# Attention's weight products 128 rows deep, with zero rows for the other head

## The chip, the cores and the metric

One core of one Trainium2 chip. The metric is the device time of one execution of the kernel in microseconds; lower is better. The time before is 529.92 us, the median of 3 runs (529.62 to 530.06).

## The reference

One layer on x of 2048 tokens by 128 features: a feed-forward part, attention, and a second feed-forward part, each with a layer norm ahead and added to x. The feed-forward part has one shared and eight routed experts of width 256, two experts chosen per token. Attention has 4 heads of 32 features and 64 slots per head. Per head, with the causal mask:

```
wk = exp(clip(slots of k));  zk = cumsum(wk over tokens)
logits = ((q k^T masked) wk) * scale / zk
p = softmax(logits over the 64 slots)
wv = exp(clip(slots of v));  zv = cumsum(wv over tokens)
A[t, s] = sum over the 64 slots m of (p / zv)[t, m] * wv[s, m],  masked
o = A v;  then o is normalised, gated and projected
```

The change concerns the line for A, "the products of the weights". All data stay float32 in this part.

## The kernel before, in words

The feed-forward parts run over experts and groups of 512 tokens. Attention lies between them and runs over 16 chunks of 128 tokens. What lies in earlier chunks is kept in a running state (logits and outputs of earlier tokens come from it), so within a chunk only 128 by 128 products are formed.

The order of work in attention is written out by hand, once per engine: each engine has a function `attn_step(i, n)` that calls the parts of up to four chunks at once, `front` (chunk i), `mid` (i - 1), `last` (i - 2) and `end` (i - 3), as `stages` gives them. Steps 0 to 3 are written out, steps 4 to 15 run in a hardware loop on each engine with two steps in its body (the branch is behind the odd step), and steps 16 to 18 are written out again. Engines meet through semaphores only, and each works off its own list in order.

The parts that matter here, with their lines:

- TensorE, in the order of a step: `project` (L1177 to 1179), `running_sums` (L1259), `turn_v` (L1250, transposes the slots of v, two heads at a time, into PSUM), `slot_logits` (L1219), `turn_o` (L1333), `weights_a` (L1311), `logits_of_earlier` (L1268), `out_proj` (L1338, waits for ScalarE's copy of o), `logits_of_chunk` (L1275), `turn_qk` (L1226 and L1230, wait for the split of q and k to be complete), `outputs` (L1323, L1325), `add_state`, `add_sums`, `scores` (L1241), `turn_p` (L1299).
- ScalarE: `copy_state` (six copies of parts of the rows, L417 and L420), `sums_log` (L394), `copy_value_slots` (L406, the transposed slots of v from PSUM to vslot_t), `sums_first_inverse` (L399), `copy_o` (L452), `qk_high` (L374, L375), `slots_high` (L362), `slots_exponent` (L355), `copy_qk_parts` (L382), `slots_middle` (L367), `soft_exp` (L431), `o_square` (L445), `copy_q` (L387), `copy_p` (L438).
- GpSimd: `rope_add` (L633, L634), `qk_low` (L640, behind L375), `slots_rest` (L617), `slots_low` (L622), `gate_o` (L648), `root_o` (L567).
- VectorE: `rope_multiply` (L870 to 875), `norm_apply` (L990), `clip_slots` (L883), `mask_a` (L953, waits for the products), `sums_product` (L899), `sums_inverse` (L904, writes slot_inv), `add_y` (L997), `soft_scale` (L912), `soft_min` (L918), `norm_shares` (L969), `soft_centre` (L926), `prob_scale` (L934), and the small rest up to `mask_s` (L891).

vslot_t and p_t hold two heads below each other: rows 0 to 63 are the slots of an even head, rows 64 to 127 those of an odd head, and the index a says which pair. `weights_a` multiplies 64 rows at a time, first both even heads, then, behind a wait of TensorE for itself (`a_even`), both odd heads. The four products go side by side into one bank of PSUM. A float32 product shows in the trace as two passes, so a step has eight loads and eight matmuls at L1311.

Of the kernel before, what the change touches and what calls it, by code (L numbers as in the profile page):

```python
# [16 lines left out]
ACT = mybir.ActivationFunctionType  # L17
# [6 lines left out]
P = 128  # L24
# [13 lines left out]
M = 64  # L38
# [49 lines left out]
def macaron_kernel(nc, x_in, consts, w_ffn, w_router, router_bias, w_qkvg, w_low, w_slots, w_out, gnorm, out):  # L88
# [3 lines left out]
    with ExitStack() as ctx:  # L92
        def sb(name, shape, dt=F32):
            return ctx.enter_context(nc.sbuf_tensor(name, shape, dt))

        def sem(name):
            return ctx.enter_context(nc.semaphore(name))
# [22 lines left out]
        zero16 = sb("zero16", [P, HM + 4 * DK], F16)  # L120
# [43 lines left out]
        state = sb("state", [P, 2, HM + 2 * 2 * DK])  # L164
# [10 lines left out]
        prob_inv = sb("prob_inv", [P, 2, H])  # L175
        pz = sb("pz", [P, HM])
        p_t = sb("p_t", [P, 2, 2, P])
        vslot_t = sb("vslot_t", [P, 2, 2, P])
        a_masked = sb("a_masked", [P, H, P])
        o1 = sb("o1", [P, D])  # L180
        o_sq = sb("o_sq", [P, D])
# [20 lines left out]
        state_ps, sum_ps, qk_ps, slots_ps, s_ps, c_ps, vturn_ps, oturn_ps = bank  # L202
# [3 lines left out]
        vslot_t_ps, pz_t_ps = vturn_ps[:, 0:HM], vturn_ps[:, HM:2 * HM]  # L206
        o_t_ps, y_ps = oturn_ps[:, 0:P], oturn_ps[:, P:2 * P]

        def stacked(q_block, k_block):
# [23 lines left out]
        whi0_done, wr_hi_done, wlo0_done = sem("whi0_done"), sem("wr_hi_done"), sem("wlo0_done")  # L233
        names = ("low_turned low_hi_done low_lo_done v_projected v_copied g_projected gate_silu gate_ready "
                 "projected slots_done clip_done slots_exp slots_b1 slots_rest slots_b2 slots_b3 rope_parts qk_done "
                 "qk_hi_done qk_lo_done qk_turned qk_t_copied q_t_copied a_even "
                 "s_done vslot_turned vslot_copied sums_done s_mask_done state_copied logits_done sums_ln sums_guess "
                 "sums_prod sums_inv back_done "
                 "logit_scaled min_done centred prob_done prob_summed pz_done pinv_done pz_turned p_copied "
# [1 line left out]
        S = {n: sem(n) for n in names.split()}  # L241
# [32 lines left out]
        def _(act):  # L274
# [126 lines left out]
            def copy_value_slots(c, p, n):  # L401

                act.wait_ge(S["vslot_turned"], c + 1)
                if n >= 2:
                    act.wait_ge(S["a_done"], c - 1)
                act.activation(vslot_t[:, p, :, :], vslot_t_ps.rearrange("p (a b) -> p a b", a=2), ACT.Copy).then_inc(S["vslot_copied"], 1)  # L406

            def copy_state(c, p, n):

# [44 lines left out]
            def attn_step(i, n):  # L454
                front, mid, last, end = stages(i, n)
                if mid:
                    copy_state(*mid)
                if mid:
                    sums_log(*mid)
                if mid:  # L460
                    copy_value_slots(*mid)
                if mid:
                    sums_first_inverse(*mid)
                if end:
                    copy_o(*end)
                if front:
                    qk_high(*front)
                if front:
                    slots_high(*front)
                if front:  # L470
                    slots_exponent(*front)
                if front:
                    copy_qk_parts(*front)
                if front:
                    slots_middle(*front)
                if mid:
                    soft_exp(*mid)
                if last:
                    o_square(*last)
                if front:  # L480
                    copy_q(*front)
                if mid:
                    copy_p(*mid)
# [46 lines left out]
        def _(pool):  # L530
# [70 lines left out]
            pool.wait_ge(wlo_done, E + 2)  # L601
            nc.gpsimd.memset(low_st[6 * LOW:P, :], 1.0).then_inc(ones_set, 1)
            pool.wait_ge(ones_set, 1)
            for zeros in (state[:, :, :], zero16[:, :]):
                nc.gpsimd.memset(zeros, 0.0)
            nc.gpsimd.tensor_copy(tri16[:, :], tri)
            nc.gpsimd.tensor_copy(rest16[:, :], rest)
# [63 lines left out]
            for g in range(NG):  # L671
                pool.wait_ge(S["gate_silu"], g + 1)
                for c in range(g * GT, (g + 1) * GT):
                    i = nc.gpsimd.tensor_tensor(gates[:, c, :], gate_raw[:, c, :], gn[:, :], ALU.mult)
# [405 lines left out]
        def _(pe):  # L1080
            mm = nc.tensor.matmul
# [220 lines left out]
            def weights_a(c, p, n):  # L1302

                pe.wait_ge(S["p_copied"], c + 1)
                pe.wait_ge(S["vslot_copied"], c + 1)
                if n >= 1:
                    pe.wait_ge(S["o1_done"], c)
                for j, done in enumerate(("a_even", "a_done")):
                    rows = slice(j * M, (j + 1) * M)
                    for a in range(2):  # L1310
                        i = mm(c_ps[:, (2 * a + j) * P:(2 * a + j + 1) * P], vslot_t[rows, p, a, :], p_t[rows, p, a, :], start=True, stop=True)  # L1311
                    i.then_inc(S[done], 1)
                    if j == 0:
                        pe.wait_ge(S["a_even"], c + 1)

            def outputs(c, p, n):

# [22 lines left out]
            def attn_step(i, n):  # L1340
# [11 lines left out]
                if last:  # L1352
                    weights_a(*last)
# [109 lines left out]
```

## Time and profile before

| | |
|---|---|
| median of 3 runs | 529.92 us |
| the profiled execution | 530.72 us |
| its span, first to last instruction | 528.8 us |
| mean granted TensorE clock | 0.957 |
| TensorE (PE) busy | 467.3 us, 88% |
| VectorE (DVE) busy | 427.0 us, 81% |
| ScalarE (ACT) busy | 309.1 us, 58% |
| GpSimd (POOL) busy | 173.3 us, 33% |
| share of L1311 in the chain that ended last | 3% |

The profile is one execution. PE is TensorE's matmuls, PEld its weight loads. Times are us from the start of the span. Busy shares are means over very different stages: attention has another limit than the feed-forward parts. A row of the timeline gives start, duration (from the first start to the last end where instructions are merged), engine, line and operation, output and inputs with their shapes, the count, and in brackets the idle time of the engine ahead of it with what ended it.

### The profile page before, as it was taken

What the parts mean: (1) busy time and instruction counts of PE and PEld (TensorE: products, weight loads), DVE (VectorE), ACT (ScalarE), POOL (GpSimd) and SP (SyncE); (2) the same over time, 40 slices, a digit from 0 to 9 for tenths busy, and PEclk for the clock granted to TensorE, in tenths of its full rate; (3) what the DMA queues carried; (4) which work ended last, traced back from release to release, by engine and by line L of the source; (5) the groups of instructions that cost most, each with busy time, mean ns of one, the idle gap of its engine ahead of it and who ended that gap; (6) DMA issues with size and microseconds to landing.
All of it is one profiled execution on the core that took longest, in us unless ns stands there. A gap on an engine that the chain in (4) does not pass through costs nothing.

```text
span 528.8 us, 12332 instructions
## 1 busy us (share of the span) xinstructions
PE 467.3 (88%) x3895; PEld 318.7 (60%) x3895; DVE 427.0 (81%) x1139; ACT 309.1 (58%) x667; POOL 173.3 (33%) x198
## 2 busy tenths in 40 slices
PE   1788999999999568998898999885889999999996
PEld 0344566666665556676776776764455666666664
DVE  3598999999999835777778777866599999999997
ACT  3543555555555675877777777653555555555553
POOL 2999960000000364566566666534000000000000
PEclk9998999999999785999999999996599999999999
DMA  6212000000000000000000000000000000000002
GB/s 204 90 61 78 1 0 0 0 0 0 0 1 1 1 1 0 2 1 2 0 0 0 0 0 0 0 1 0 2 1 2 0 0 0 0 0 0 0 0 79
DMA packets 6697, 6.98 MB, mean 13 GB/s; under 512 B 818, under 2 KB 5170, under 8 KB 6676
## 3 DMA queue, kind: packets, MB, share of 16 engines
q1 hardware_dynamic: 6532, 6.33, 3.9%
q10 hardware_dynamic: 144, 0.39, 0.2%
q8 instruction: 11, 0.18, 0.1%
q14 instruction: 10, 0.08, 0.1%
HBM read 5.67 MB, written 1.05 MB: 13 GB/s over the span
## 4 chain that ended last, share of the span: by engine, by line
PE 60%; DVE 19%; issue 9%; ACT 7%; POOL 2%; DVEq 1%; DMA 1%; POOLq 0%; ACTq 0%
PE bank L1128 15%; PE bank L1140 10%; PE bank L1141 10%; PE bank L1142 10%; DVE h L804 4%; PE bank L1311 3%; DVE h_lo L810 2%; ACT gate_s L313 2%; PE bank L1325 2%; PE bank L1275 2%; DVE stats L702 2%; DVE pz L934 1%; DVE x L793 1%; DVE logit_c L926 1%; PE bank L1230 1%
## 5 line engine op out<-in xcount | busy, mean ns | idle before, releaser
L318 ACT ACTIVATE h_hi<-h 128x512 f16<-128x512 f32 x144 | 90.7, 630 | 133.3 <-DVE h L804 133.3
L804 DVE SCALAR_TENSOR_TENSOR h<-bank,gate_s 128x512 f32<-128x512 f32 x144 | 99.4, 690 | 28.4 <-ACT gate_s L313 19.0
L1128 PE MATMUL bank<-w_hi,h_hi 128*128 (+1 forms) x576 | 106.4, 221 | 12.9 <-DVE h_lo L810 8.3
L1140 PE MATMUL bank<-xt_hi,w_hi 128*128 128x512 f16 x288 | 111.8, 388 | 0.0
L1141 PE MATMUL bank<-xt_hi,w_lo 128*128 128x512 f16 x288 | 111.7, 388 | 0.0
L1142 PE MATMUL bank<-xt_lo,w_hi 128*128 128x512 f16 x288 | 111.5, 387 | 0.0
L1128 PE MATMUL bank<-w_hi,h_lo 128*128 (+1 forms) x576 | 105.9, 221 | 0.0
L1128 PE MATMUL bank<-w_lo,h_hi 128*128 (+1 forms) x576 | 105.9, 221 | 0.0
L810 DVE TENSOR_TENSOR h_lo<-h,h_hi 128x512 f16<-128x512 f32 x144 | 100.6, 698 | 0.1
L793 DVE SCALAR_TENSOR_TENSOR x<-bank,wts,x 128x128 f32<-128x128 f32 x288 | 86.5, 343 | 1.6 <-PE bank L1128 1.1
L313 ACT ACTIVATE gate_s<-bank 128x512 f32<-128x512 f32 x144 | 83.5, 580 | 0.6 <-PE bank L1142 0.6
L1128 PEld LDWEIGHTS bank<-w_hi,h_hi 128*128 128x128 f16 x576 | 56.6, 98 | 37.4 <-DVE h_lo L810 12.1
L1128 PEld LDWEIGHTS bank<-w_lo,h_hi 128*128 128x128 f16 x576 | 56.8, 99 | 12.4 <-issue 0.3
L1128 PEld LDWEIGHTS bank<-w_hi,h_lo 128*128 128x128 f16 x576 | 56.9, 99 | 0.0
L1142 PEld LDWEIGHTS bank<-xt_lo,w_hi 128*128 (+1 forms) x288 | 28.7, 100 | 35.6 <-issue 3.0
L538 POOL TENSOR_SCALAR var_e<-mv 128x4 f32<-128x4 f32 x12 | 3.4, 284 | 117.9 <-issue 95.1
L1140 PEld LDWEIGHTS bank<-xt_hi,w_hi 128*128 (+1 forms) x288 | 28.7, 100 | 19.5 <-issue 2.5
L1141 PEld LDWEIGHTS bank<-xt_hi,w_lo 128*128 (+1 forms) x288 | 28.7, 100 | 19.0 <-issue 2.2
L953 DVE TENSOR_TENSOR a_masked<-bank,cst 128x512 f32<-128x512 f32 x16 | 11.1, 692 | 20.6 <-PE bank L1311 20.6
L617 POOL TENSOR_TENSOR slot_r<-slots,slot_b 128x512 f32<-128x512 f32 x16 | 23.8, 1485 | 6.7 <-issue 6.3
L622 POOL TENSOR_TENSOR slot_b<-slot_r,slot_b 128x512 bf16<-128x512 f32 x16 | 20.5, 1282 | 15.8 <-ACT slot_b L367 15.8
L382 ACT ACTIVATE qk_t<-bank 96x1024 f16<-96x1024 f16 x16 | 16.3, 1019 | 15.9 <-PE bank L1230 15.9
(159 smaller groups left out, 855.7 us busy)
## 6 DMA issues: line engine op xcount, KB each, us to landing
wf<-in_w_ffn SPq DMA_DIRECT2D x8, 384.0 KB, 3.1
x<-in_x SPq DMA_DIRECT2D x4, 256.0 KB, 4.9
out_dram<-x SPq DMA_DIRECT2D x4, 256.0 KB, 2.3
cst<-in_consts SPq DMA_DIRECT2D x1, 455.0 KB, 5.3
wf<-in_w_ffn ACTq DMA_DIRECT2D x1, 384.0 KB, 4.2
wqkvg<-in_w_qkvg SPq DMA_DIRECT2D x1, 256.0 KB
wslots<-in_w_slots SPq DMA_DIRECT2D x3, 64.0 KB
wo<-in_w_out SPq DMA_DIRECT2D x1, 64.0 KB
```

Source lines behind the costliest of these rows:

```text
L313: act.activation(gate_s[:, ih, :], gate_ps[ih][:, :], ACT.Silu, scale=1.0 / (XS * WS)).then_inc(silu_done, 1)
L318: act.activation(h_hi[:, g, ih, :], h32[:, ih, :], ACT.Copy).then_inc(hhi_done, 1)
L382: act.activation(qk_t[0:STACK, p, :, :], qk_t_ps[0:STACK, :].rearrange("p (a t) -> p a t", a=2 * H), ACT.Copy).then_inc(S["qk_t_copied"], 1)
L617: nc.gpsimd.tensor_tensor(slot_r[:, :], slots[:, p, :], slot_b1[:, p, :], ALU.subtract).then_inc(S["slots_rest"], 1)
L622: nc.gpsimd.tensor_tensor(slot_b3[:, p, :], slot_r[:, :], slot_b2[:, p, :], ALU.subtract).then_inc(S["slots_b3"], 1)
L793: i = nc.vector.scalar_tensor_tensor(x[:, t, :], down_ps[j][:, c % 2 * P:(c % 2 + 1) * P], wts[:, t, e:e + 1] if isinstance(e, int) else w ...
L804: nc.vector.scalar_tensor_tensor(h32[:, ih, :], up_ps[ih][:, :], HS / (XS * WS), gate_s[:, ih, :], ALU.mult, ALU.mult).then_inc(hmul_done, 1)
L810: nc.vector.tensor_tensor(h_lo[:, g, ih, :], h32[:, ih, :], h_hi[:, g, ih, :], ALU.subtract).then_inc(hlo_done, 1)
L1128: i = mm(dst, hp[:, g, ih, c * P:(c + 1) * P], wcols(wp, e, at, D), start=(k == 0), stop=(k == 3 * IH - 1))
L1140: mm(ps[:, :], wcols(w_hi, e, at, P), xt_hi[:, ts], start=True, stop=False)
L1141: mm(ps[:, :], wcols(w_lo, e, at, P), xt_hi[:, ts], start=False, stop=False)
L1142: mm(ps[:, :], wcols(w_hi, e, at, P), xt_lo[:, ts], start=False, stop=True).then_inc(done, 1)
```

## The change

vslot_t gets one more index j, the head of the pair: each head has its own 128 rows by 128 columns, with its 64 rows filled and the 64 rows of the other head zero. The zeros are written once, by GpSimd, before attention. ScalarE copies each half of the rows into its place, by two instructions where one was. The products take all 128 rows of vslot_t and of p_t; rows of the other head add zeros. The wait between even and odd heads and its semaphore are gone. The order of the calls on all engines is unchanged.

```diff
-        vslot_t = sb("vslot_t", [P, 2, 2, P])
+        vslot_t = sb("vslot_t", [P, 2, 2, 2, P])
...
-                act.activation(vslot_t[:, p, :, :], vslot_t_ps.rearrange("p (a b) -> p a b", a=2), ACT.Copy).then_inc(S["vslot_copied"], 1)
+                for j in range(2):
+                    rows = slice(j * M, (j + 1) * M)
+                    i = act.activation(vslot_t[rows, p, :, j, :], vslot_t_ps[rows, :].rearrange("p (a b) -> p a b", a=2), ACT.Copy)
+                i.then_inc(S["vslot_copied"], 1)
...
-            for zeros in (state[:, :, :], zero16[:, :]):
+            for zeros in (state[:, :, :], zero16[:, :], vslot_t[:, :, :, :, :]):
                 nc.gpsimd.memset(zeros, 0.0)
...
-                for j, done in enumerate(("a_even", "a_done")):
-                    rows = slice(j * M, (j + 1) * M)
-                    for a in range(2):
-                        i = mm(c_ps[:, (2 * a + j) * P:(2 * a + j + 1) * P], vslot_t[rows, p, a, :], p_t[rows, p, a, :], start=True, stop=True)
-                    i.then_inc(S[done], 1)
-                    if j == 0:
-                        pe.wait_ge(S["a_even"], c + 1)
+                for a in range(2):
+                    for j in range(2):
+                        i = mm(c_ps[:, (2 * a + j) * P:(2 * a + j + 1) * P], vslot_t[:, p, a, j, :], p_t[:, p, a, :], start=True, stop=True)
+                i.then_inc(S["a_done"], 1)
```

## Rows read from the trace of the kernel before

**Rows 1.** The page, costliest groups: busy, mean ns, idle before, releaser.

```profile
L953 DVE TENSOR_TENSOR a_masked<-bank,cst 128x512 f32<-128x512 f32 x16 | 11.1, 692 | 20.6 <-PE bank L1311 20.6
```

**Rows 2.** Timeline of TensorE in one step of attention, 298 to 303.5 us.

```profile
298.00 0.20 PEld L1299 LDWEIGHTS bank<-cst,pz 128*128 128x128 f32 x2 [0.41 <-DVE pz L934]
...
300.25 0.14 PEld L1333 LDWEIGHTS bank<-cst,o 128*128 128x128 f32 x1 [0.79 <-DVE o L990]
...
300.51 0.52 PEld L1311 LDWEIGHTS bank<-p_t,vslot_t 64*128 64x128 f32 x4
...
301.28 0.52 PEld L1311 LDWEIGHTS bank<-p_t,vslot_t 64*128 64x128 f32 x4 [0.25 <-PE bank L1311]
...
301.91 0.30 PEld L1268 LDWEIGHTS bank<-state,q_t 128*128 128x128 f32 x2
...
302.24 0.41 PEld L1338 LDWEIGHTS bank<-wo,o_t 128*128 128x128 f32 x2
...
303.40 0.20 PEld L1226 LDWEIGHTS bank<-cst,qk 128*128 128x128 f32 x1
```

**Rows 3.** Timeline of ScalarE in the same step.

```profile
299.64 0.45 ACT L420 ACTIVATE state<-bank 64x64 f32<-64x64 f32 x2
...
300.60 0.38 ACT L406 ACTIVATE vslot_t<-bank 128x256 f32<-128x256 f32 x1
300.87 0.63 ACT L399 ACTIVATE slot_i<-slot_ln 128x512 f32<-128x512 f32 x1
...
301.39 0.28 ACT L452 ACTIVATE o_t<-bank 128x128 f32<-128x128 f32 x1
```

**Rows 4.** Timeline of VectorE and GpSimd, this step and the next.

```profile
302.02 0.69 DVE L953 TENSOR_TENSOR a_masked<-bank,cst 128x512 f32<-128x512 f32 x1 [1.23 <-PE bank L1311]
...
302.35 0.67 POOL L640 TENSOR_TENSOR qk_parts<-qk,qk_parts 128x256 f16<-128x256 f32 x1 [1.41 <-ACT qk_parts L375]
...
303.35 0.69 DVE L904 SCALAR_TENSOR_TENSOR slot_inv<-slot_zi,slot_i 128x512 f32<-128x512 f32 x1
...
312.05 0.67 POOL L640 TENSOR_TENSOR qk_parts<-qk,qk_parts 128x256 f16<-128x256 f32 x1 [1.34 <-ACT qk_parts L375]
...
313.10 0.69 DVE L904 SCALAR_TENSOR_TENSOR slot_inv<-slot_zi,slot_i 128x512 f32<-128x512 f32 x1
```

**Rows 5.** Timeline where slot_inv meets an operation of GpSimd, four steps.

```profile
205.97 0.67 POOL L640 TENSOR_TENSOR qk_parts<-qk,qk_parts 128x256 f16<-128x256 f32 x1 [2.20 <-ACT qk_parts L375]
206.08 1.11 DVE L904 SCALAR_TENSOR_TENSOR slot_inv<-slot_zi,slot_i 128x512 f32<-128x512 f32 x1
...
206.69 0.18 PEld L1226 LDWEIGHTS bank<-cst,qk 128*128 128x128 f32 x1 [0.57 <-POOL qk_parts L640]
...
234.99 0.69 DVE L904 SCALAR_TENSOR_TENSOR slot_inv<-slot_zi,slot_i 128x512 f32<-128x512 f32 x1
235.01 1.69 POOL L617 TENSOR_TENSOR slot_r<-slots,slot_b 128x512 f32<-128x512 f32 x1 [0.42 <-issue]
...
254.36 1.15 POOL L617 TENSOR_TENSOR slot_r<-slots,slot_b 128x512 f32<-128x512 f32 x1 [0.42 <-issue]
254.42 1.64 DVE L904 SCALAR_TENSOR_TENSOR slot_inv<-slot_zi,slot_i 128x512 f32<-128x512 f32 x1
...
332.47 1.70 DVE L904 SCALAR_TENSOR_TENSOR slot_inv<-slot_zi,slot_i 128x512 f32<-128x512 f32 x1
```

**Rows 6.** Instructions of line L420, 220 to 330 us: duration in ns, min/median/max.

```profile
L420 ACT ACTIVATE state<-bank x24: 217/218/219, 221.6 to 328.9; 64x64 f32<-64x64 f32 x24
```

**Rows 7.** The chain that ended last: start, length, second halves of L1311.

```profile
252.35 0.72 PE bank L1311 x4
...
262.65 0.71 PE bank L1311 x4
...
291.71 0.71 PE bank L1311 x4
```

**Rows 8.** Timeline of GpSimd ahead of attention.

```profile
73.41 0.74 POOL L605 MEMSET state<- 128x768 f32 x1
```

More of the change, by code:

```diff
@@ L235, in macaron_kernel @@
                  "projected slots_done clip_done slots_exp slots_b1 slots_rest slots_b2 slots_b3 rope_parts qk_done "
-                 "qk_hi_done qk_lo_done qk_turned qk_t_copied q_t_copied a_even "
+                 "qk_hi_done qk_lo_done qk_turned qk_t_copied q_t_copied "
                  "s_done vslot_turned vslot_copied sums_done s_mask_done state_copied logits_done sums_ln sums_guess "
```

## The prediction

> **What bounds the kernel now.** I read the page's groups first, then the waits, the chain, and the middle of attention instruction by instruction. The two feed-forward parts share no instruction with the change, so only attention (about 197 to 368 us) matters. There VectorE loses 20.6 us, 16 times, waiting for the products of the weights (L1311) [rows 1]. That wait is real, but ask what is late next once it shrinks.
>
> I take the step from 300.2 us as the pattern. TensorE: transpose of o at 300.25, products with even heads at 300.51, odd heads at 301.28, query product at 301.91, projection L1338 at 302.24, transposes of q and k (L1226) at 303.40 [rows 2]. ScalarE runs the copy of vslot_t at 300.60, the inverse guess at 300.87, the copy of o at 301.39, without a gap [rows 3]. Behind them in the same queue are the two splits of q and k, and they release GpSimd's L640 at 302.35, 0.67 long, which ends at 303.02 [rows 4]. L1226 needs L640 and starts 0.38 us after it. So two paths run side by side: one over L1311, and ScalarE's queue with L640, which has only 0.38 us to spare. Where TensorE does wait for L640, it starts 0.05 us after its end (206.64 to 206.69) [rows 5], so 0.33 us are usable.
>
> **What the change takes from TensorE.** Today L1333's load to L1268's load is 301.91 - 300.25 = 1.66 us [rows 2]. Two transposes in a row load 0.06 apart (0.20 for two of 0.14, L1299), and the four loads of a half take 0.52 with 0.19 for one, a pitch of 0.11. Afterwards: 0.06 + 8 x 0.11 = 0.94, so 0.72 us less. The pieces: about 0.33 for the wait on a_even between the halves (301.28 instead of 300.51 + 0.44), and 0.20 each for going from 128 rows to 64 and back, where the next load comes 0.2 later than that pitch although its data are long there. The matmuls themselves cost the same: 8 passes of the same 128 columns. The result is earlier by less, since the drain behind it doesn't count: the last load goes from 301.28 + 0.33 = 301.61 to 300.25 + 0.06 + 0.77 = 301.08, so the mask of a starts 0.52 us earlier, at 301.50 instead of 302.02 [rows 4].
>
> **What it adds to ScalarE.** One copy (0.38 long, the next instruction starts 0.27 behind it [rows 3]) becomes two of 64 rows with the same 256 columns. No row has that shape, so I bound it. Lower end: they overlap as full-height copies do, 0.27 more. Upper end: no overlap at all. The nearest rows are L420, also two halves of 64 rows out of PSUM: two of 0.218 take 0.45 [rows 3, 6], so each begins only when the one before has ended. By them the pair takes 0.38 + 0.39 and two gaps of 0.015, 0.80 instead of 0.27. I take +0.53 us per step, the value of the nearest row, and keep 0.27 for the range.
>
> The Trainium skill (ScalarE: Activation LUTs, What ACT_TABLE_LOAD costs) says that activations back to back overlap by about 93 ns. The halves of L420 don't do that here; by that rule the price of the pair would be about 0.3 and the sum that of the rival *Faster* below, not the one I forecast.
>
> **What that does to the step.** The copy of o ends at 301.39 + 0.28 + 0.53 = 302.20, so L1338 can load at 302.25: where it is today (302.24). TensorE's 0.72 us are gone at that instruction. Then the second delay: L640 starts at 302.88 and ends at 303.55, and L1226 loads at 303.60 instead of 303.40. Each such step is 0.20 us longer. In the steps behind the loop's branch slot_inv stands 1.05 behind L640 (313.10 to 312.05) where it stands 1.00 behind it at 303.35 to 302.35 [rows 4]; the branch gives ScalarE 0.05 us more room, and they lose 0.15.
>
> **The race between VectorE and GpSimd.** slot_inv (L904) and GpSimd's operations on SBUF exclude each other. L640 started first at 205.97 and slot_inv took 1.11 instead of 0.69; at 254.36 L617 was first by 0.06 and slot_inv took 1.64. At 234.99 slot_inv was first, by only 0.02, and L617 took 1.69 instead of 1.15 [rows 5]. Who starts first wins, and the loser waits out the winner. Now the distance: slot_inv moves forward by 0.52 with the mask, L640 back by 0.53, so 1.00 becomes -0.05: **slot_inv goes first** and L640 waits. L617 ended 1.02 behind slot_inv then, 0.13 less than it takes alone. So slot_inv ends at 302.83 + 0.69 = 303.52, L640 at 303.52 + 0.67 - 0.13 = 304.06, L1226 loads at 304.10: 0.70 us later than today. Behind the branch the distance is 1.05 - 1.05 = 0.00, a tie; I give it to GpSimd.
>
> **The sum.** Thirteen steps (3 to 15) have front, mid and last; six of them (4, 6 to 14) follow a branch. 7 x 0.70 + 6 x 0.15 = +5.8. In steps 1 and 2 TensorE already waits for L640 [rows 5], so they pay the whole 0.53 twice: +1.1. In steps 16 and 17 there is no L640; the products are on the chain, and give 0.52 in the last and some 0.4 in the other (estimate): -0.9. Twice today, at 254.42 and 332.47, slot_inv loses against L617 [rows 5]; such a step has 262.65 - 252.35 = 10.30 us where its like has 301.28 - 291.71 = 9.57 [rows 2, 7]. With slot_inv 0.52 earlier and L617 0.53 later that can't happen: 2 x 0.73 = -1.4. The new zeros cost GpSimd about 1 us (0.74 for 768 columns [rows 8], now 1024 more) near 74 us, hidden in its idle time up to attention; were that gone, 1 us. One semaphore wait less costs nothing. Total +4.5 us. The profiled execution took 530.72 (span 528.8), the median is 529.92; 4.5 on top of the median is 534.4.
>
> **Rivals.**
> - *Forecast, 0.33:* slot_inv beats L640 in seven steps: 534.4.
> - *The race is lost everywhere, 0.20:* the tie also goes to VectorE; 13 x 0.70 = 9.1, 9.1 + 1.1 - 0.9 - 1.4 = +7.9: 537.8. It takes 0.03 us.
> - *L640 wins everywhere, 0.25:* 0.05 us the other way, for example if the load behind L1333 isn't pulled forward. Then 7 x 0.20 + 6 x 0.15 = 2.3, total +1.1: 531.0.
> - *Faster, 0.17:* the two copies overlap, +0.27. L1226 then loads at 303.02 + 0.27 + 0.05 = 303.34, 0.06 earlier than today, 0.11 behind a branch: -1.1. With +0.5 for steps 1 and 2, -0.9 and -1.4: -2.9, 527.0. It decides from a price under 0.33 per pair on. Full-height neighbours speak for it, L420 against it.
> - *The change doesn't do what it says, 0.05:* the gaps around L1311 have another reason than the number of rows and stay. Then the mask moves by about 0.33 only, L640 wins as above, and ScalarE's delay is all that is left: about 531.
>
> **How the numbers follow.** A measurement tells 0.2%, 1.06 us, from no change. Slower by more: 0.33 + 0.20, and half of the cases at +1.1 (0.30): 0.68. Same: the other half, 0.15. Faster: 0.17. The likeliest case alone spans 532.5 to 536 (price of the pair 0.50 to 0.56, tail 0.5 either way, one or two steps changing sides). The range for 8 in 10 takes in the three slower cases and leaves out most of the overlap case: 528.5 to 538.2.
>
> **What would show it.** Right: eight loads of L1311 in about 0.97 us without a gap; 0.77 to 0.82 us from the first half copy to the inverse guess; TensorE idle before L1338 for ScalarE's copy of o, and before L1226 for L640; the mask's wait down from 1.2 us to about 0.7; L640 at 1.2 us in every second step, slot_inv at about 1.2 in the others; L617 at 1.15 more often. Wrong: the inverse guess only 0.55 behind the first half copy; no L640 over 0.7; a gap still ahead of or behind L1311; steps shorter than 9.6 us.

## The result, and the profile after

The changed kernel takes 537.38 us (median of 4 runs, 537.03 to 538.99); the kernel before had 529.99 (529.62 to 532.25, 4 runs). The ratio is 1.0136, 95% interval 1.0102 to 1.0171. It is slower by 7.4 us, where +4.5 was forecast: inside the range, on the forecast side, and nearly at the 537.8 of the rival in which the race is lost everywhere.

The page of the changed kernel: its span, the engines' busy time, the chain by engine, and costliest groups (columns as in [rows 1]).

```profile
span 535.0 us, 12349 instructions
PE 463.4 (87%) x3895; PEld 316.1 (59%) x3895; DVE 428.4 (80%) x1139; ACT 318.5 (60%) x683; POOL 173.9 (32%) x199
PE 55%; DVE 16%; ACT 14%; issue 10%; POOL 3%; DMA 1%; DVEq 0%; ACTq 0%; POOLq 0%
L643 POOL TENSOR_TENSOR qk_parts<-qk,qk_parts 128x256 f16<-128x256 f32 x16 | 15.3, 955 | 31.7 <-ACT qk_parts L375 31.7
```

TensorE is less busy than before and its share of the chain went from 60% to 55%; ScalarE's doubled, from 7% to 14%. GpSimd's low part of q and k (line 640 before, 643 now) has grown from 0.67 to 0.96 us in the mean. The lines of the engines between the edits are three higher than before.

The wait for the products, by the same group as in [rows 1]:

```profile
L956 DVE TENSOR_TENSOR a_masked<-bank,cst 128x512 f32<-128x512 f32 x16 | 11.1, 691 | 12.7 <-PE bank L1313 12.7
```

It fell from 20.6 to 12.7 us, 0.5 us in each of 16 steps: what the change aimed at happened, and the kernel is slower all the same. The same step as in [rows 2 to 4], from the timeline of the changed kernel:

```profile
304.87 0.14 PEld L1333 LDWEIGHTS bank<-cst,o 128*128 128x128 f32 x1 [0.79 <-DVE o L993]
304.94 0.97 PEld L1313 LDWEIGHTS bank<-p_t,vslot_t 128*128 128x128 f32 x8
305.23 0.76 ACT L408 ACTIVATE vslot_t<-bank 64x256 f32<-64x256 f32 x2
305.82 0.30 PEld L1271 LDWEIGHTS bank<-state,q_t 128*128 128x128 f32 x2
306.01 0.63 ACT L399 ACTIVATE slot_i<-slot_ln 128x512 f32<-128x512 f32 x1
306.13 0.69 DVE L956 TENSOR_TENSOR a_masked<-bank,cst 128x512 f32<-128x512 f32 x1 [0.72 <-PE bank L1313]
306.67 0.28 ACT L455 ACTIVATE o_t<-bank 128x128 f32<-128x128 f32 x1
306.99 0.30 PEld L1338 LDWEIGHTS bank<-wo,o_t 128*128 128x128 f32 x2 [0.86 <-ACT o_t L455]
307.46 0.69 DVE L907 SCALAR_TENSOR_TENSOR slot_inv<-slot_zi,slot_i 128x512 f32<-128x512 f32 x1
307.63 1.05 POOL L643 TENSOR_TENSOR qk_parts<-qk,qk_parts 128x256 f16<-128x256 f32 x1 [2.06 <-ACT qk_parts L375]
...
308.73 0.14 PEld L1229 LDWEIGHTS bank<-cst,qk 128*128 128x128 f32 x1 [0.55 <-POOL qk_parts L643]
```

From L1333 to the query product TensorE needs 305.82 - 304.87 = 0.95 us instead of 1.66, eight loads without a gap. Then it stands for 0.86 us before the projection, waiting for ScalarE's copy of o, and for 0.55 us before the transposes of q and k, waiting for L640 (now L643). slot_inv started 0.17 us ahead of L640, and L640 was held: it took 1.05 us instead of 0.67. From the load of L1333 to that of the transposes it is 3.86 us; it was 3.15.

### The profile page after: what moved, and what is told of

The parts are those of the page before. It is cut to its first block, busy times and chain, and to the rows that moved or that the text cites. A ratio compares the mean times of both kernels' runs of the same rounds, so it can differ in the third digit from the quotient of the medians.

```text
span 535.0 us, 12349 instructions
## 1 busy us (share of the span) xinstructions
PE 463.4 (87%) x3895; PEld 316.1 (59%) x3895; DVE 428.4 (80%) x1139; ACT 318.5 (60%) x683; POOL 173.9 (32%) x199
## 3 DMA queue, kind: packets, MB, share of 16 engines
HBM read 5.67 MB, written 1.05 MB: 13 GB/s over the span
## 4 chain that ended last, share of the span: by engine, by line
PE 55%; DVE 16%; ACT 14%; issue 10%; POOL 3%; DMA 1%; DVEq 0%; ACTq 0%; POOLq 0%
PE bank L1131 15%; PE bank L1143 9%; PE bank L1145 9%; PE bank L1144 9%; DVE h L807 4%; DVE h_lo L813 2%; DVE pz L937 2%; PE bank L1325 2%; ACT gate_s L313 2%; ACT slot_ln L394 2%; DVE stats L705 2%; ACT state L420 1%; PE bank L1233 1%; ACT slot_b L362 1%; DVE x L796 1%
## 5 line engine op out<-in xcount | busy, mean ns | idle before, releaser
L813 DVE TENSOR_TENSOR h_lo<-h,h_hi 128x512 f16<-128x512 f32 x144 | 102.2, 710 | 0.1
L643 POOL TENSOR_TENSOR qk_parts<-qk,qk_parts 128x256 f16<-128x256 f32 x16 | 15.3, 955 | 31.7 <-ACT qk_parts L375 31.7
L382 ACT ACTIVATE qk_t<-bank 96x1024 f16<-96x1024 f16 x16 | 16.3, 1020 | 14.9 <-PE bank L1233 14.9
L1098 PE MATMUL bank<-cst,xn 128*128 128x128 f32 x48 | 12.2, 415 | 13.1 <-ACT xn L290 13.1
```

Source lines behind the costliest of these rows:

```text
L382: act.activation(qk_t[0:STACK, p, :, :], qk_t_ps[0:STACK, :].rearrange("p (a t) -> p a t", a=2 * H), ACT.Copy).then_inc(S["qk_t_copied"], 1)
L643: nc.gpsimd.tensor_tensor(stacked(2, 1), qk[:, p, :].rearrange("p (a h d) -> p a h d", a=2, h=H), stacked(0, 0), ALU.subtract).then_inc(S[ ...
L813: nc.vector.tensor_tensor(h_lo[:, g, ih, :], h32[:, ih, :], h_hi[:, g, ih, :], ALU.subtract).then_inc(hlo_done, 1)
```

## The experiments

All against the kernel before on the same chip. "Attention" is the time from the first to the last load of L1333 in the profiled execution (143.8 us before), which leaves out what the feed-forward parts add in scatter. The last column leaves out the last step as well, from the last load but one to the last (135.1 us before).

| run | us, median | ratio (95%) | attention, us | less its last step |
|---|---|---|---|---|
| changed kernel | 537.4 | 1.0136 (1.0102 to 1.0171) | 149.7 | 141.5 |
| e1 two half copies alone | 533.5 | 1.0057 (1.0024 to 1.0091) | 145.8 | 137.0 |
| e2 copy cut by columns | 529.7 | 0.9986 (0.9966 to 1.0006) | 142.4 | 133.6 |
| e3 deep products, one copy | 523.9 | 0.9877 (0.9848 to 0.9905) | 136.2 | 127.9 |
| e4 self-wait put back | 535.1 | 1.0102 (1.0049 to 1.0155) | 146.3 | 136.9 |
| e5 slot_inv waits for L640 | 533.8 | 1.0064 (1.0033 to 1.0094) | 145.2 | 136.9 |
| e6 odd half by VectorE | 525.2 | 0.9907 (0.9877 to 0.9938) | 136.0 | 127.7 |
| e7 changed kernel, copy late | 520.4 | 0.9812 (0.9787 to 0.9837) | 134.3 | 126.1 |
| e8 kernel before, copy late | 541.6 | 1.0203 (1.0168 to 1.0238) | 153.0 | 143.0 |
| e9 halves swapped | 535.2 | 1.0093 (1.0058 to 1.0127) | 147.0 | 138.7 |
| e10 e8 with the race ordered | 530.2 | 1.0006 (0.9985 to 1.0027) | 143.8 | 134.1 |

The last step is left out because TensorE's clock differs there from one profiled execution to the next. In its first 3 us the granted clock was 1.00 in the kernel before and 0.80 in the changed one, but 0.57 in e4, 0.52 in e8 and 0.59 in e10, close to the lower of its two levels (1.2 GHz against 2.4). The same eight passes of L1311 there, in the kernel before and in e8:

```profile
357.63 1.48 PE L1311 MATMUL bank<-p_t,vslot_t 64*128 64x128 f32 x8
```
```profile
368.21 2.50 PE L1311 MATMUL bank<-p_t,vslot_t 64*128 64x128 f32 x8
```

Up to there the clock was 0.99 or 1.00 between the loads in all twelve traces. Why it falls earlier in some executions is open.

### The two parts, each alone: e1 and e3

e1 is the kernel before with this edit:

```diff
-                act.activation(vslot_t[:, p, :, :], vslot_t_ps.rearrange("p (a b) -> p a b", a=2), ACT.Copy).then_inc(...)
+                for j in range(2):
+                    rows = slice(j * M, (j + 1) * M)
+                    i = act.activation(vslot_t[rows, p, :, :], vslot_t_ps[rows, :].rearrange("p (a b) -> p a b", a=2), ACT.Copy)
+                i.then_inc(S["vslot_copied"], 1)
```

Expected:

> The kernel before with one edit: the copy of vslot_t is two instructions of 64 rows, products and layout as before. Theory (the pair costs ScalarE 0.53 us because halves with another first row don't overlap; the rest of the slowdown is L640 losing its race): the distance from L640 to slot_inv goes from 1.00 to 0.47, L640 stays at 0.67 us in all steps, the transposes of q and k start 0.15 to 0.20 later, and the two steps lost to L617 are gone: 530.0 + 2.3 + 1.1 - 1.4 = 532.0 (531 to 533.5). Rival 'ScalarE's delay is the whole slowdown': 537. Rival 'the halves overlap': pair to next instruction 0.53 to 0.60 in all, time 529 to 530.

Measured: 533.5, at the upper end. Its timeline, and the durations (ns, min/median/max) of L640, here line 643, from 220 to 350 us:

```profile
302.54 0.76 ACT L408 ACTIVATE vslot_t<-bank 64x256 f32<-64x256 f32 x2
303.32 0.63 ACT L399 ACTIVATE slot_i<-slot_ln 128x512 f32<-128x512 f32 x1
303.97 0.28 ACT L455 ACTIVATE o_t<-bank 128x128 f32<-128x128 f32 x1
```
```profile
L643 POOL TENSOR_TENSOR qk_parts<-qk,qk_parts x13: 672/673/676, 225.8 to 344.6; 128x256 f16<-128x256 f32 x13
```

The pair puts the inverse guess at 0.78 behind its first half, as forecast. But the copy of o comes 0.65 behind the guess, not the 0.52 of [rows 3]: 0.13 us that no term of the sum had. L640 is never held, and ScalarE's delay alone is not the slowdown. slot_inv is: it starts only 0.33 to 0.49 us behind L640 and takes 0.74 to 0.89 us in steps 3 to 15. That costs next to nothing: the steps take 10.03 and 9.78 us by turns, against 10.01 and 9.77 in e5 below, where slot_inv always takes 0.69.

e3 is the changed kernel with its pair of copies undone:

```diff
-                for j in range(2):
-                    rows = slice(j * M, (j + 1) * M)
-                    i = act.activation(vslot_t[rows, p, :, j, :], vslot_t_ps[rows, :].rearrange("p (a b) -> p a b", a=2), ACT.Copy)
+                i = act.activation(vslot_t[:, p, :, 0, :], vslot_t_ps.rearrange("p (a b) -> p a b", a=2), ACT.Copy)
```

> The changed kernel with one copy of all 128 rows by 256 columns into the places j = 0; it leaves out the separation of the two heads (the places j = 1 stay zero), so that the products are priced without ScalarE's part. Theory: L1333's load to L1268's load 0.95 us, mask 0.52 us earlier, the transposes of q and k wait for L640 and start 0.33 to 0.38 earlier, L640 stays at 0.67 (distance 0.48): 530.0 - 4.6 - 1.4 - 0.9 = 523 (521.5 to 525). Rival 'the deeper products bring nothing, or were hidden': 529 to 530.5.

Measured: 523.9 and attention 7.6 us shorter. About 1.5 of that are the two lost races, as e2 will show, so the deep products are a gain of some 6 us wherever ScalarE doesn't pay for them; they were not hidden.

In attention the pair alone costs 2.0 us and the deep products alone give 7.6; together they cost 5.9. The two parts don't add up because the step has two paths side by side: with the pair in place TensorE waits for ScalarE and loses its gain, and the race comes on top.

### What a second instruction costs ScalarE: e2 and e9

e2, on the kernel before:

```diff
-                act.activation(vslot_t[:, p, :, :], vslot_t_ps.rearrange("p (a b) -> p a b", a=2), ACT.Copy).then_inc(...)
+                for a in range(2):
+                    i = act.activation(vslot_t[:, p, a, :], vslot_t_ps[:, a * P:(a + 1) * P], ACT.Copy)
+                i.then_inc(S["vslot_copied"], 1)
```

> The kernel before with one edit: the copy of vslot_t is two instructions of all 128 rows and 128 columns each. Theory (overlap is lost only where the first row changes): the inverse guess starts 0.31 to 0.36 us behind the first of the two, instead of 0.27 for one and 0.78 for two halves of the rows; hidden in the 0.33 us of slack: 529.5 to 530.5. Rival 'every second instruction costs its whole length': 0.5 us and more, 531 to 533.

The timeline of e2:

```profile
303.47 0.44 ACT L407 ACTIVATE vslot_t<-bank 128x128 f32<-128x128 f32 x2
303.78 0.64 ACT L399 ACTIVATE slot_i<-slot_ln 128x512 f32<-128x512 f32 x1
304.30 0.29 ACT L454 ACTIVATE o_t<-bank 128x128 f32<-128x128 f32 x1
```

0.31 us for two, 0.27 for one: cutting the copy by columns costs 0.04 us, cutting it by rows 0.51. The two are not the same work: cut by columns each instruction takes 128 columns, cut by rows 256. Had the halves overlapped like full-height copies, the pair would still have cost the 0.27 of the forecast's lower end, so about 0.24 us are the two lost overlaps. The count of instructions doesn't lose them, since both overlaps in e2 are 0.11 to 0.13 us. Nor does the height: in e6 below ScalarE copies rows 0 to 63 alone, and the inverse guess overlaps that half by 0.10. What is left is the change of the first row. In attention, e2 is 1.4 us faster than the kernel before (1.6 without the last step); slot_inv took 0.69 us in all of its steps 3 to 15, so this is what two lost races cost, as the forecast has it. In the whole (529.7) that stays inside the interval.

e9, on the changed kernel:

```diff
-                for j in range(2):
+                for j in (1, 0):
```

> The changed kernel with the two half copies in the other order: rows 64 to 127 first, rows 0 to 63 second. In the changed kernel the copy of o starts 0.65 us behind the inverse guess, where it is 0.52 in the kernel before and with one copy. Theory 'the lost overlap behind the inverse guess comes from the half that starts at row 64 being just ahead': it is back at 0.52, L640 starts 0.13 us earlier, the distance to slot_inv goes from -0.17 and -0.12 to about 0.0, L640 wins in some steps: 533.5 to 536.5. Rival 'it comes from having two instructions': still 0.65, L640 held in all steps, 537.4 unchanged. In both the pair itself keeps its price, since the first rows change twice either way.

The timeline of e9, ScalarE:

```profile
305.50 0.77 ACT L408 ACTIVATE vslot_t<-bank 64x256 f32<-64x256 f32 x2
306.18 0.62 ACT L399 ACTIVATE slot_i<-slot_ln 128x512 f32<-128x512 f32 x1
306.70 0.26 ACT L455 ACTIVATE o_t<-bank 128x128 f32<-128x128 f32 x1
```

and slot_inv with L640 in two steps that follow each other:

```profile
297.93 0.67 POOL L643 TENSOR_TENSOR qk_parts<-qk,qk_parts 128x256 f16<-128x256 f32 x1 [1.86 <-ACT qk_parts L375]
298.10 1.05 DVE L907 SCALAR_TENSOR_TENSOR slot_inv<-slot_zi,slot_i 128x512 f32<-128x512 f32 x1
...
307.60 0.69 DVE L907 SCALAR_TENSOR_TENSOR slot_inv<-slot_zi,slot_i 128x512 f32<-128x512 f32 x1
307.65 1.18 POOL L643 TENSOR_TENSOR qk_parts<-qk,qk_parts 128x256 f16<-128x256 f32 x1 [1.94 <-ACT qk_parts L375]
```

The 0.52 is back. The lost overlap has moved: the first half, at row 64, now starts 0.03 us after the end of the logarithm ahead of it (L394), and the guess overlaps the second half, at row 0. L640 now starts 0.04 us behind slot_inv in every second step and is held there; in the others it is ahead, by 0.05 to 0.10 in most and by 0.17 in the one shown. That is the picture which the forecast drew for the changed kernel (-0.05 and 0.00), and a time near its 534.4 (535.2). Those 0.13 us decide the race.

### The race itself: e4, e5, e8 and e10

e4 makes TensorE wait for itself in the middle of the changed kernel's products:

```diff
                     for j in range(2):
                         i = mm(c_ps[:, (2 * a + j) * P:(2 * a + j + 1) * P], vslot_t[:, p, a, j, :], p_t[:, p, a, :], start=True, stop=True)
+                    if a == 0:
+                        i.then_inc(S["a_even"], 1)
+                        pe.wait_ge(S["a_even"], c + 1)
```

> The changed kernel with a wait of TensorE for itself put back in the middle of its eight passes (behind the second product). Theory: the mask of a and with it slot_inv come 0.33 us later, which puts L640 ahead of slot_inv by 0.25 to 0.3 us in every step; L640 is back at 0.67 us and the time FALLS by about 0.5 us in 11 steps: 537.4 - 5.8 = 531.6 (530.5 to 533). Rival 'no race, ScalarE's delay alone': no change, or slower by up to 14 x 0.33 = 4.6: 537 to 542.

e5 puts one wait ahead of slot_inv in the changed kernel:

```diff
                 dve.wait_ge(S["sums_prod"], c + 1)
+                if n < NC - 1:
+                    dve.wait_ge(S["qk_lo_done"], c + 2)
```

> The changed kernel with one wait more: slot_inv on VectorE waits until GpSimd's L640 of the same step is done. Theory: L640 takes 0.67 us in every step, the transposes of q and k start 0.50 us earlier than in the changed kernel, slot_inv starts about 0.8 us later and has room for it: 531.6 (530.5 to 533). Rival 'no race': the added wait gives nothing or costs, 537 to 542.

Durations of L640 (line 643), 220 to 350 us, in the changed kernel, in e4 and in e5:

```profile
L643 POOL TENSOR_TENSOR qk_parts<-qk,qk_parts x13: 671/1052/1148, 225.6 to 348.5; 128x256 f16<-128x256 f32 x13
```
```profile
L643 POOL TENSOR_TENSOR qk_parts<-qk,qk_parts x13: 668/671/674, 226.0 to 344.7; 128x256 f16<-128x256 f32 x13
```
```profile
L643 POOL TENSOR_TENSOR qk_parts<-qk,qk_parts x13: 669/670/676, 227.5 to 346.2; 128x256 f16<-128x256 f32 x13
```

Either wait, each of which can only delay, shortens attention, by 3.4 and 4.5 us; without the last step, in which e4's clock was low, by 4.6 in both. The whole times (535.1 and 533.8) fall too, by 2.3 and 3.6; for e4 alone the intervals overlap with the changed kernel's, so there the verdict rests on the durations and on attention. They stay 3.5 and 2.2 us above what I expected. 1.2 of that is a wrong price: I had put the race at about 0.5 us in each of 11 steps, 5.8 in all, but a held L640 took 1.05 or 1.14 us instead of 0.67, which makes 4.6. Another 1.2 in e4 is its last step (9.40 us against 8.20). The rest lies outside attention and was not looked into.

e4 also prices the change of depth. Its loads:

```profile
302.39 0.14 PEld L1336 LDWEIGHTS bank<-cst,o 128*128 128x128 f32 x1 [0.80 <-DVE o L993]
...
302.46 0.52 PEld L1313 LDWEIGHTS bank<-p_t,vslot_t 128*128 128x128 f32 x4
...
303.24 0.52 PEld L1313 LDWEIGHTS bank<-p_t,vslot_t 128*128 128x128 f32 x4 [0.25 <-PE bank L1313]
303.68 0.30 PEld L1271 LDWEIGHTS bank<-state,q_t 128*128 128x128 f32 x2
```

With the self-wait kept, the products start 0.07 behind L1333 instead of 0.26, and the query product follows the second half by 0.44 instead of 0.63 [rows 2]: 0.19 us at each change between 64 and 128 rows, gone with the change. The Trainium skill (TensorEngine Tiling (Array Packing), Key Properties) says that changing the tiling mode drains the engine; the traces agree in that each change costs time, 0.19 us; what the engine does in it they don't show.

e8 takes the kernel before and moves its one copy in ScalarE's order; e7 below makes the same move in the changed kernel:

```diff
                 if mid:
                     sums_log(*mid)
-                if mid:
-                    copy_value_slots(*mid)
...
                 if front:
                     slots_exponent(*front)
+                if mid:
+                    copy_value_slots(*mid)
```

> The kernel before with the copy of vslot_t (one instruction) moved behind the exponentials as in the run beside it. Theory of the race: the exponentials end 0.27 us earlier, GpSimd's L617 then starts about 0.18 us AHEAD of slot_inv in every step, slot_inv takes 1.6 instead of 0.69 us, and every step costs what two cost in the kernel before: 13 x 0.73 - 1.4 = +8: 538 (535 to 539.5). Rival 'no race, TensorE's path is the bound': unchanged, 529.5 to 530.5.

The timeline of e8:

```profile
310.95 1.16 POOL L617 TENSOR_TENSOR slot_r<-slots,slot_b 128x512 f32<-128x512 f32 x1 [0.42 <-issue]
310.98 1.68 DVE L904 SCALAR_TENSOR_TENSOR slot_inv<-slot_zi,slot_i 128x512 f32<-128x512 f32 x1
...
313.52 1.16 POOL L622 TENSOR_TENSOR slot_b<-slot_r,slot_b 128x512 bf16<-128x512 f32 x1 [1.42 <-ACT slot_b L367]
...
313.75 1.21 DVE L926 TENSOR_TENSOR logit_c<-logit,logit_min 128x256 f32<-128x256 f32 x1
```

Work that ends earlier makes the kernel slower, by 11.6 us in the medians: L617 comes 0.03 us ahead of slot_inv, slot_inv takes 1.68 instead of 0.69, and behind it the centring of the logits loses its race too (1.21 instead of 0.42). The lost races are 7.9 of these us, the difference of attention without the last step, where 8 were expected. 1.3 us more lie in the last step, 9.96 us between loads of L1333 instead of 8.69 (357.37 to 366.06), with the clock at 0.52. The rest lies outside attention: the first transposes of q and k load at 201.58 us in e8 and at 198.21 in the kernel before, and anywhere from 197.34 to 202.16 in the twelve traces, though the edits leave the work ahead of them alone but for the zeros.

e10 adds to e8:

```diff
                 if n >= 1:
                     pool.wait_ge(S["slots_b3"], c)
+                    pool.wait_ge(S["sums_inv"], c)
```

> The kernel before with the late copy (541.6 measured) and one wait more: GpSimd's L617 waits until VectorE's slot_inv of the same step is done. Theory (those 11.6 us are the lost race alone): slot_inv is back at 0.69 us in every step, L617 at 1.15 starting 0.9 us later, and TensorE's path is the bound again: 530.0 less the two lost races of the kernel before, 1.4: 528.6 (528 to 530.5). Rival 'the late copy itself costs, for example by delaying ScalarE's copy of the transposed q and k': 533 or more.

Measured: 530.2 over 10 runs, 11.4 us less than e8. In attention, the last step left out, one wait takes back 8.9 us, the 7.9 of e8 and 1.0 more, so those were the race and the late copy costs nothing by itself. The 1.4 us below the kernel before that I expected show there as that 1.0; in the whole they don't show, since its last step is long as well, 9.66 us, at a clock of 0.59.

### Versions that beat both: e6 and e7

e6 gives the odd half to VectorE, in the changed kernel:

```diff
+            def copy_odd_slots(c, p, n):
+                dve.wait_ge(S["vslot_turned"], c + 1)
+                if n >= 2:
+                    dve.wait_ge(S["a_done"], c - 1)
+                nc.vector.tensor_copy(vslot_t[M:P, p, :, 1, :], vslot_t_ps[M:P, :].rearrange("p (a b) -> p a b", a=2)).then_inc(S["vslot_odd"], 1)
...
+                if mid:
+                    copy_odd_slots(*mid)
                 if last:
                     mask_a(*last)
```

ScalarE keeps rows 0 to 63, and TensorE waits for both semaphores where it waited for one.

> The changed kernel, but rows 64 to 127 of vslot_t are copied by VectorE, between the clipping and the mask of a, where it waits for the products. Theory: ScalarE's 0.53 us are gone (next instruction 0.25 to 0.30 behind its one half), VectorE's 0.4 us fit its wait, L640 stays at 0.67: about 523 (521.5 to 525.5), faster than both kernels. Rival 'VectorE has no room': mask later by up to 0.4 us per step, 526 to 531.

Measured: 525.2. VectorE's copy takes 0.43 us in its wait for the products, and the inverse guess follows ScalarE's half by 0.27.

e7 is the changed kernel with the late copy.

> The changed kernel with ScalarE's copy of vslot_t moved behind the exponentials (L355), ahead of its wait for the transposes of q and k. Nothing needs the copy before the end of the step. Theory: the splits of q and k come 0.80 us earlier than in the changed kernel, L640 is ahead of slot_inv by 0.7 and its end before slot_inv's start, TensorE's 0.72 us come through nearly whole: about 521 (519 to 524). Rival 'the copy's place is indifferent, its cost is what counts': 537.

Its timeline, around the step at 294 us:

```profile
294.39 0.97 PEld L1313 LDWEIGHTS bank<-p_t,vslot_t 128*128 128x128 f32 x8
...
295.66 0.35 PEld L1338 LDWEIGHTS bank<-wo,o_t 128*128 128x128 f32 x2
...
296.30 0.67 POOL L643 TENSOR_TENSOR qk_parts<-qk,qk_parts 128x256 f16<-128x256 f32 x1 [1.28 <-ACT qk_parts L375]
296.64 0.62 ACT L355 ACTIVATE slots<-clipped 128x512 f32<-128x512 f32 x1
296.90 0.69 DVE L907 SCALAR_TENSOR_TENSOR slot_inv<-slot_zi,slot_i 128x512 f32<-128x512 f32 x1
297.02 0.14 PEld L1229 LDWEIGHTS bank<-cst,qk 128*128 128x128 f32 x1
297.16 0.75 ACT L408 ACTIVATE vslot_t<-bank 64x256 f32<-64x256 f32 x2
```

Measured: 520.4 us, 9.6 below the kernel before and 17.0 below the changed one, by moving one call. The pair costs as much as ever (0.75 us) but runs while ScalarE waits for the transposes; L640 starts 0.60 us ahead of slot_inv, and in this step TensorE has no idle time ahead of L1338 or of the transposes.

## Why the prediction came out as it did

- *TensorE's gain: right.* 0.72 forecast, 0.71 measured; the mask starts 1.26 us behind L1333's load, 1.25 forecast. The split into 0.33 for the wait and 0.20 at each change of depth is shown by e4. The gain ends at the projection, as forecast: 0.86 us of wait for the copy of o.
- *The pair of copies: right in kind, a term too small.* 0.78 us from the first half to the inverse guess (0.80 forecast), and e2 and e6 show that the change of the first row takes the overlap, not the count or the height. **The step that failed** is "I take +0.53 us per step": the instruction behind the inverse guess lost its overlap too, and the price up to L640 is 0.65: L640 starts 2.40 us behind the first half (307.63 to 305.23) where it started 1.75 behind the one copy (302.35 to 300.60 in [rows 3, 4]).
- *The race: right in kind, its count wrong through that term.* With 0.65 the distance from L640 to slot_inv is 1.00 - 0.52 - 0.65 = -0.17, as measured. Behind the branch that sum gives -0.12 and the traces have -0.07 to -0.08, since the products start 0.03 us later there: no tie either. L640 was held in 11 of 13 steps, not in 7. The two others, at 256.49 and 317.98, are those in which the products themselves started 0.20 us behind L1333 instead of 0.07 to 0.10 and took the mask with them; why is open. So the rival at 537.8 came true, but for the two steps; 0.03 us were said to decide it, and 0.13 did. With the 0.13 taken back (e9) the forecast's own case is there.
- *The price of a lost race.* 0.70 us per step forecast; the held steps take 10.40 or 10.25 us where 9.75 and 9.57 were usual, +0.65 and +0.68. That is close by two errors that cancel: ScalarE's delay is 0.26 or 0.20 of it (e5 against the kernel before) where 0.20 or 0.15 was forecast, and the race itself, against e5, where neither slot_inv nor L640 is held, 0.39 or 0.48 where 0.50 was forecast.
- *Steps 1 and 2.* +1.1 forecast, +1.3 measured between the transposes of the first and the third chunk.
- *The end.* -0.9 forecast, hardly met. From the load of L1333 in step 16 to the last it was 17.06 us (349.00 to 366.06); the changed kernel has these:

```profile
355.70 0.14 PEld L1333 LDWEIGHTS bank<-cst,o 128*128 128x128 f32 x1 [0.85 <-DVE o L993]
364.33 0.14 PEld L1333 LDWEIGHTS bank<-cst,o 128*128 128x128 f32 x1 [1.81 <-DVE o L993]
372.53 0.18 PEld L1333 LDWEIGHTS bank<-cst,o 128*128 128x128 f32 x1 [3.55 <-DVE o L993]
```

  16.83 us, 0.23 less. The last step gave its 0.5 (with the clock at 0.80 in its first 3 us), the one ahead of it paid for ScalarE's pair: 8.63 us instead of 8.37, where e3, without the pair, has 7.98.
- *The two lost races of the kernel before are gone: right.* L617 takes 1.15 us in all 13 steps, and e2 puts the pair of them at 1.4 us.
- *The zeros: right.* GpSimd's new operation takes 0.96 us at 73.88 and delays nothing that shows: the first transposes of q and k load at 197.48 us, 198.21 before.
- *The sum.* Between the loads of L1333: 11 x 0.66 + 2 x 0.2 = 7.7, less 1.5, less 0.2, makes 6.0; measured 149.7 - 143.8 = 5.9. Both sides come from the same two traces, so this says that no term is missing, not that each is right. With 1.3 for steps 1 and 2 it is 7.2, and the medians differ by 7.4.

Open: what in ScalarE ties the overlap to the first row, and why the loss reaches one instruction further here when the half at row 64 comes last. That both happen is measured; the cause isn't. A half at row 64 is not enough for the second: in the same step of the changed kernel the state's last half, at row 64 too, is followed by the logarithm (L394), and the copy behind that (L408) overlaps it by 0.10 us; in e7 the two instructions behind the pair (L382, L367) overlap by 0.10 as well. It shows only between the inverse guess and the copy of o.

## What to carry to other kernels

Before an edit that trades one engine's time for another's, write down the distance between each pair of VectorE and GpSimd operations that exclude each other: when the edit moves both, its effect can be many times its own size, and an added wait that fixes the order can be a gain. Then look for the place in the paying engine's list where it stands idle anyway; here the same work was worth +7.4 us in one place and -9.6 in another, and the kernel before, with only the second place, lost 11.6, of which 7.9 were shown to be a race that one wait wins back.

## What the runs showed of the hardware

- slot_inv and GpSimd's two-input operations exclude each other by order of start, down to 0.02 us, as in this step of the changed kernel, where the products came late:

```profile
256.49 0.67 POOL L643 TENSOR_TENSOR qk_parts<-qk,qk_parts 128x256 f16<-128x256 f32 x1 [1.99 <-ACT qk_parts L375]
256.51 1.19 DVE L907 SCALAR_TENSOR_TENSOR slot_inv<-slot_zi,slot_i 128x512 f32<-128x512 f32 x1
```

  The Trainium skill (SBUF — State Buffer, Who interferes with whom) says so for a VectorE instruction with two inputs from SBUF against a GpSimd instruction that reads SBUF; the traces agree, and slot_zi, which has one input in PSUM, was never held.
- Activations that follow each other without a wait and start at the same row overlap by 0.09 to 0.13 us; where the first row changes the next starts 0.01 to 0.03 us after the end. One pair with the same first row, the copy of o behind the inverse guess in the changed kernel, e1, e4 and e5, doesn't overlap either. The page on ScalarE in the Trainium skill (ScalarE: Activation LUTs, What ACT_TABLE_LOAD costs) gives an overlap of 93 ns for back-to-back activations without this exception; here the measurement decides: 128 rows by 256 columns cost 0.04 us more when they are cut by columns and 0.51 more when cut by rows, some 0.24 of it for the two lost overlaps.
- Going from 128 rows to 64 on TensorE costs 0.19 us, and again on the way back, each more than half of the 0.33 that the wait between the halves cost.
- What a lost race costs depends on the room of the one that is held. slot_inv, held for 0.05 to 0.37 us in steps 3 to 15 of e1 and e4, left the steps within 0.02 us of those of e5; held for 0.83 to 0.99 us in e8 it cost 0.72 to 0.76 per step, with the centring behind it. L640, held for 0.38 to 0.47 us, cost 0.39 to 0.48, since the transposes of q and k wait for it.
